# Sixteen expert groups worked in between the heads, and their routing packed into 24 heads

## The reference

```python
xn = layernorm(x)
# attention: 16 heads of 128, causal
q, k, v = xn @ Wq + bq, xn @ Wk + bk, xn @ Wv + bv
att = softmax(q k^T / sqrt(128) + causal) v      ;  att @ Wo + bo
# mixture of experts: 64 experts, the best 6 per token, at most 128 tokens per expert
scores = sigmoid(xn @ w_gate); idx = top_k(scores, 6); w = scores[idx] / sum
pos = running count of the token in its expert, over all tokens in order
x_disp[e, pos] = xn            # dropped from position 128 on
out_r = (silu(x_disp @ w_up_g) * (x_disp @ w_up_v)) @ w_down
shared = (silu(g_s) * y_s) @ w_shared_down
out = x + att + shared + sum_k w[k] * out_r[idx[k], pos[k]]
```

## Time and profile before

| | |
|---|---|
| median of three runs | 1820.65 us (1816.66 to 1821.87) |
| the profiled execution | 1822.72 us |
| its span in the trace | 1821.0 us |
| PE busy | 1690.2 us, 93% |
| DVE busy | 1368.7 us, 75% |
| ACT busy | 1085.7 us, 60% |
| POOL busy | 1122.1 us, 62% |
| mean granted PE clock | 0.956 |

### The profile page before, as it was taken

How to read it: one execution, slowest core, us unless ns; L and a number is a source line. 1 busy time by engine, 2 the same in 40 slices (tenths; PEclk the granted TensorE clock), 3 DMA queues, 4 the chain that set the end, 5 groups by cost and what they waited for, 6 DMA issues and landing times. The chain is left out here.

```text
span 1821.0 us, 49686 instructions
## 1 busy us (share of the span) xinstructions
PE 1690.2 (93%) x19217; PEld 1315.9 (72%) x19217; DVE 1368.7 (75%) x3128; ACT 1085.7 (60%) x2347; POOL 1122.1 (62%) x1006
## 2 busy tenths in 40 slices
PE   4699999999999999999986779999998999999997
PEld 3477767777777777777665667777776777777775
DVE  8677777777677777777663446888888888888885
ACT  2566666665566666666661227666666666666664
POOL 0257757776676777776660006777777677777763
PEclk7799999999999999999997669999999999999998
DMA  9377667765656665656656656778988789898976
GB/s 372 112 152 131 121 120 128 135 112 101 120 94 101 96 106 95 96 95 101 115 99 160 206 160 119 138 142 141 164 140 159 122 141 165 139 143 136 163 129 113
DMA packets 686658, 245.04 MB, mean 135 GB/s; under 512 B 637456, under 2 KB 674721, under 8 KB 685536
## 3 DMA queue, kind: packets, MB, share of 16 engines
q1 hardware_dynamic: 657472, 197.83, 61.6%
q0 software_dynamic: 18432, 33.64, 7.7%
q10 hardware_dynamic: 10528, 10.49, 1.8%
HBM read 57.11 MB, written 50.46 MB: 59 GB/s over the span
## 5 line engine op out<-in xcount | busy, mean ns | idle before, releaser
L485 POOL TENSOR_TENSOR prob<-prob 128x128 f16<-128x128 f32 (+7 forms) x512 | 653.0, 1280 | 576.1 <-ACT prob L874 569.2
L867 ACT ACTIVATE prob<-prob,nmax 128x128 f32<-128x128 f32 (+7 forms) x512 | 396.8, 775 | 530.4 <-DVE prob L1312 514.3
L708 PE MATMUL ps_s<-kT,qT 128*128 128x512 f16 (+3 forms) x2304 | 459.7, 327 | 4.3 <-DVE prob L1312 4.3
L723 PE MATMUL ps_o<-probT,vh 128*128 128x256 f16 (+1 forms) x3840 | 428.3, 265 | 7.2 <-DMA probT<-prob 7.2
L1312 DVE TENSOR_SCALAR_CACHE_REDUCE prob<-ps_s,neg_scale 128x128 f32<-128x128 f32 (+7 forms) x512 | 412.2, 809 | 14.3 <-PE ps_s L710 10.6
L723 PEld LDWEIGHTS ps_o<-probT,vh 128*128 128x128 f16 x3840 | 368.7, 99 | 53.5 <-issue 9.1
L874 ACT CAST prob<-prob 128x128 f16<-128x128 f32 (+7 forms) x512 | 341.5, 667 | 2.3
L708 PEld LDWEIGHTS ps_s<-kT,qT 128*128 128x128 f16 x2304 | 201.9, 98 | 144.7 <-issue 4.3
L1341 DVE SCALAR_TENSOR_TENSOR resid<-ps_y,yscale,resid 128x256 f32<-128x256 f32 x512 | 223.0, 477 | 11.6 <-PE ps_y L737 5.8
L737 PE MATMUL ps_y<-wo,oT 128*128 128x256 f16 x1536 | 210.6, 273 | 22.2 <-DVE oT L1327 20.4
L599 PEld LDWEIGHTS ps_t<-xT,wq 128*128 128x128 f16 x6144 | 205.1, 100 | 24.6 <-issue 9.8
(11 more groups left out here) (182 smaller groups left out, 1651.6 us busy)
## 6 DMA issues: line engine op xcount, KB each, us to landing
dispatched<-zeros SPq DMA_DIRECT2D x16, 512.0 KB, 14.1
probT<-prob SPq DMA_TRANSPOSE x512
ex<-dispatched SPq DMA_DIRECT2D x16, 512.0 KB, 4.3
expert_out<-eo ACTq DMA_DIRECT2D x16, 512.0 KB, 3.7
eup<-in_L_ffn_w_up_dram SPq DMA_DIRECT2D x64, 64.0 KB, 2.1
dispatched<-xn,slot_idx POOLq DMA_INDIRECT x192
xn_columns<-xnth SPq DMA_DIRECT2D x24, 128.0 KB
got<-expert_out,slot_idx POOLq DMA_INDIRECT x192
```

The costliest lines, as they stand in the source:

```text
L485: pool.tensor_tensor(low_cols(j), prob_cols(j).rearrange("p (r k) -> p r k", k=P), high_cols(j), ALU.subtract).then_inc(p_low, 1)
L708: pe.matmul(s_cols(j, lo, hi), qT[:, u, a, j * P:(j + 1) * P], kT[:, u, c, lo:hi], start=(n == 0), stop=(n == 2 and hi < w))
L723: mm = pe.matmul(ps_o[:, lo:2 * P], vh[:, u, a, r * D:(r + 1) * D], probT[:, PT_AT[c] + 2 * r + s, lo:], start=(r + n == 0), stop=(r == 2 ...
L867: nc.scalar.activation(prob_cols(j), prob_cols(j), ACT.Exp, bias=nmax[:, j:j + 1], scale=-1.0, accum_out=rsum[:, i % 2, j:j + 1]).then_inc ...
```

## The change

The loop of its own for the experts goes away, on all engines; every engine calls `attention(0, B * H)` once. `early(i)` and `later(i)` place the work: group pair e = i - 27 starts in head i, and ends in head i + 1.

```diff
-        ROWS = 2 * NP
-        SPLIT = ROWS + 2
+        ROWS = 3 * NP // 2
+        NGR = E // EG
+        EX0 = ROWS + 3
+        GA0 = EX0 + NGR // 2 + 1
         def even_part(i):
-            return i // 2 if i % 2 == 0 and i < ROWS else -1
+            return 2 * (i // 3) + i % 3 if 0 <= i < ROWS and i % 3 < 2 else -1
         def odd_part(i):
-            return i // 2 if i % 2 == 1 and i < ROWS else -1
+            return 2 * (i // 3) + i % 3 - 1 if 0 <= i < ROWS and i % 3 > 0 else -1
...
+        def early(i):
+            return i - EX0 if EX0 <= i < EX0 + NGR // 2 else -1
+        def later(i):
+            return i - EX0 if EX0 < i <= EX0 + NGR // 2 else -1
```

PE's order in the expert heads (lines without a + stood there before):

```diff
                     scores(i, 1)
+                    if later(i) >= 0:
+                        hidden_columns(i, 2 * later(i) - 2)
+                        up_project(i, 2 * later(i) - 1)
...
                         project_y(i - 1, 1)
+                    if early(i) >= 0:
+                        rows_to_columns(i, 2 * early(i), 0)
+                    if old:
                         values(i - 1, 2)
                     scores(i, 3)
+                    if early(i) >= 0:
+                        rows_to_columns(i, 2 * early(i), 1)
...
                         project_y(i - 1, 2)
+                    if even_part(i) >= 0 and even_part(i) % 2:
+                        transpose_rows(i, even_part(i))
+                    if mid_part(i) >= 0:
+                        shared_down(i, mid_part(i))
+                    if later(i) >= 0:
+                        down_project(i, 2 * later(i) - 2, 0)
+                        down_project(i, 2 * later(i) - 2, 1)
...
                     scores(i, 5)
+                    if later(i) >= 0:
+                        hidden_columns(i, 2 * later(i) - 1)
+                    if early(i) >= 0:
+                        up_project(i, 2 * early(i))
+                        rows_to_columns(i, 2 * early(i) + 1, 0)
...
                     scores(i, 6)
+                    if later(i) >= 0:
+                        down_project(i, 2 * later(i) - 1, 0)
...
                     scores(i, 7)
+                    if early(i) >= 0:
+                        rows_to_columns(i, 2 * early(i) + 1, 1)
+                    if later(i) >= 0:
+                        down_project(i, 2 * later(i) - 1, 1)
```

The new PE functions borrow PSUM from the attention, and wait for it. Three of the four `rows_to_columns` halves write ps_y, which `project_y` uses:

```diff
+            def rows_to_columns(i, n, h):
+                dst = ps_t[:, 0, :] if n % 2 + h == 0 else ps_y[:]
+                if n % 2 + h:
+                    pe.wait_ge(y_added, NC * (i - 1) + 2 * (n % 2) + h + 1)
...
+            def hidden_columns(i, n):
+                pe.wait_ge(eh_ready, n + 1)
+                if n % 2:
+                    pe.wait_ge(eo_d, n)
+                else:
+                    pe.wait_ge(y_added, NC * (i - 1) + 1)
...
+            def down_project(i, n, h):
+                bank = (n + h) % 2
+                if n % 2 == 0:
+                    free_bank(i, bank)
...
+                pe.matmul(ps_t[:, bank, :], ehT[two, n % 2, :], edn[two, :], start=True, stop=True).then_inc(ed_done, 1)
```

More of the change, by code:

```diff
@@ L257, in causal_attention_with_moe @@
         eo_d = sem("eo_d")
-        eo_stored = sem("eo_stored")
+        eo_out = [sem(f"eo_out{h}") for h in range(2)]
         gathered = [sem(f"gathered{u}") for u in range(2)]
@@ L627, in project_v @@
                 h = i % H
+                if half == 0 and early(i) >= 0 and not turn(i, more):
+                    pe.wait_ge(eta_ready, 2 * early(i) + 1)
                 if i == 0 and half == 0:
@@ new lines, in up_project @@
+            def up_project(i, n):
+                if n % 2:
+                    pe.wait_ge(y_added, NC * (i - 1) + 1)
+                elif n:
+                    pe.wait_ge(eo_d, n - 1)
+                else:
+                    free_bank(i, 1)
+                pe.wait_ge(eup_in, 16 * EG * (n + 1))
+                pe.wait_ge(eta_ready, n + 1)
+                pe.wait_ge(etd_ready, n + 1)
+                dst = ps_y[:, 2 * P:] if n % 2 else ps_t[:, 1, 2 * P:]
+                for e in range(EG):
+                    for k in range(KC):
+                        mm = pe.matmul(dst[:, e * 2 * HE:(e + 1) * 2 * HE], exT[:, e, k, :], eup[:, e, k, :],
+                                       start=(k == 0), stop=(k == KC - 1))
+                mm.then_inc(eu_done, 1)
@@ L729, in project_y @@
                 pe.wait_ge(o_low, m + 1)
+                if c == 0 and early(i) >= 0:
+                    pe.wait_ge(etd_ready, 2 * early(i) + 2)
+                if c == 1 and later(i + 1) >= 0:
+                    pe.wait_ge(eht_ready, 2 * later(i + 1) - 1)
+                    pe.wait_ge(eu_taken, 2 * later(i + 1))
+                if c == 2 and early(i + 1) >= 0:
+                    pe.wait_ge(etd_ready, 2 * early(i + 1) + 1)
+                if c == 3 and early(i + 1) >= 0:
+                    pe.wait_ge(eta_ready, 2 * early(i + 1) + 2)
                 if m:
@@ L972, in attention @@
                         high_q(i + 1, 1)
+                    if later(i) >= 0:
+                        gate_of_hidden(2 * later(i) - 1)
+                    if early(i) >= 0 and i > EX0:
+                        load_expert_rows(2 * early(i) + 1)
                     softmax_exp(i, 2)
@@ L975, in attention @@
                         high_weights(3)
+                    if early(i) >= 0:
+                        first_columns(2 * early(i))
                     if old:
@@ L1401, in attention @@
                         low_q(i + 1, 1)
-                    if late >= 0:
-                        slot_indices(late)
+                    if later(i) >= 0:
+                        hidden(2 * later(i) - 1)
+                    if i == EX0 - 1:
+                        gate_weights()
+                    if slot_part(i) >= 0:
+                        slot_indices(slot_part(i))
                     if odd >= 0:
@@ L1432, in attention @@
                         add_y(i - 1, 2, mixed(4))
+                    if even >= NC and even % 2:
+                        low_columns(even)
+                    if mid_part(i) >= 0:
+                        add_shared(mid_part(i), NC * (i - 1) + 3)
+                    if later(i) >= 0:
+                        second_outputs(2 * later(i) - 2)
+                    if old:
                         low_o(i - 1, 3)
@@ L1438, in attention @@
                         low_k(i + 1, 0)
-                    if even >= NC:
+                    if early(i) >= 0:
+                        hidden(2 * early(i))
+                    if even >= NC and even % 2 == 0:
                         low_columns(even)
@@ L1449, in attention @@
                     block_max(i, 7)
+                    if early(i) >= 0:
+                        second_columns(2 * early(i) + 1)
+                    if later(i) >= 0:
+                        second_outputs(2 * later(i) - 1)
                     mix_at(7)
```

490 lines of the change are left out of this document (266 added, 224 removed).

## The result

The changed kernel takes 1873.41 us (median of 4 runs, 1871.78 to 1876.38), the kernel before 1819.89 beside it: a ratio of 1.030, 95% interval 1.028 to 1.032. It is slower, as forecast, but 42 us over the forecast of 1831 and 17 beyond the range's end. The profiled execution took 1872.88 us with a span of 1871.1; 1872.88 - 1822.72 = 50.2 us have to be explained.

A forecast was written before the change was run, and what follows sets the result against it. PE was taken to be full wherever there are heads, leaving room only in the expert phase, drain and refill. Terms -135.9 + 73 + 33 - 4 + 24 + 18 + 2 = +10.1 gave 1831 us median, range 1796 to 1856.

The forecast's parts named there:

- Term 1: Heads 33 and 34 with the expert phase between: drain, expert work and refill go, -135.9 us.
- Terms 2 and 3: Expert heads: the experts' own PE time returns, +73 us; new in-order PE waits, mostly for DVE, +33 us.
- Point (2): Heads 28 to 34 take 36.6 us plus a clock drop each, some 38; under 34 refutes the added waits.
- Point (3): PE idles ahead of a transposing matmul reading ex, released by DVE, 2 to 3 us, seven or eight times.
- The turn at head 31: Head 31 already waits for columns; the 2.5 us wait and added transposes lie under that transfer, -4 us.
- Terms 4 and 5: Routing in 24 heads: new PE waits, +24 us (-8 to +45); some 12 clock drops, +18 us (0 to 30).
- term 6: Additions, gathers and statistics: a ninth addition per head hidden by slack, statistics squeezed into six heads; +2 us.
- Point (5): Clock entries of 0.5 in the expert heads and triples of routing heads, 10 to 16 of them.
- Rival 1: The clock holds: same waits, but no drop follows; -18, 1813 us; chance 0.17.
- The lock on DVE: `hidden`, with both operands in SBUF, may be slowed while POOL works; 0.3 us taken, 0 to 1.5 per head.
- Rival 2: Waits for add_y and low_v are hidden: 1756 us with none, 1781 with a third; chance 0.15.
- Rival 3: Longer chains: two more us in each of 9 expert and 16 routing heads, less catch-up, +25, 1856 us; chance 0.18.

The follow-up runs named there:

- experiment 3: Changed kernel, but PE issues 32 unused products ahead of the wait for POOL's normalised rows in six routing heads; 1850.79 us, ratio 1.0198.
- experiment 1: Changed kernel, but POOL normalises an odd pair's two tiles behind low_probs 1 and 2 instead of 2 and 3; 1846.75 us, ratio 1.0143.
- the fastest variant: Three-edit kernel of experiment 6, plus ACT copying v and odd pairs' columns earlier and DVE taking low_v earlier; 1776.31 us, ratio 0.9792.
- Experiment 5: Changed kernel, but routing as in the kernel before, experts behind heads 35 to 43, twelve additions per late head; 1829.23 us, ratio 1.0061.
- experiment 6: Changed kernel with POOL's normalise earlier, shared down product behind values, odd group's hidden rows later, and add_shared ahead of add_y(i-1, 2); 1806.76 us, ratio 0.9932.

## Why the prediction was wrong, point by point

**Term 1, the phase (-135.9): right.** No long stretch at low clock is left.

**Terms 2 and 3, the expert heads (+73 and +33): right.** The nine heads cost 115.3 more than plain ones; four drops at 1.6 are 6.5 of it, which leaves 35.8 for the waits beside the 73 of work. Point (2) said 36.6 us for a full head and 38 with a drop: 36.66 and 38.2 to 38.9. Point (3): 2.3 us seven times where I had 2.5. Behind scores 1 it is 0.6 as worked out, behind scores 7 0.7 for 1.1; heads 27 and 35 wait for more than the 4 together. That the total of a full head came out to 0.1 is in part luck: PE waits for 3.6 where I had 4.2, and its own time is larger by about as much (33.05 us busy, against 23.50 + 9.1). All waits of the nine heads in the trace add up to 31.6, so some 4 us of the 35.8 are not waits.

**The turn at head 31 (-4): right.** A turn cost 4.2 above its neighbours (30.03 against 25.86); it now takes 38.55 against 38.25.

**Terms 4 and 5, routing (+24) and the clock (+18): here the forecast broke.** The sum was +10, measured are +50. Routing cost 70.4 + 4.2 (the turn's saving is in the 70.4) = 74.6 us, of which I split off the clock as follows. Between heads 1 and 35 the trace has 105.8 us at half clock, as much as 31 stretches of 3.41; 27 of them lie in routing heads. The price of one is 1.6 (38.25 - 36.66), of two running together 2.4 to 2.85 (experiment 3): by this estimate some 38 us (36 to 40) in routing heads, less 3 for the two that the kernel before had there, and 6.5 in expert heads. So term 4 proper is 74.6 - 35 = 40 in place of 26 (with the 2 of term 6 for statistics), and term 5 is some 41 in place of 18. The miss of 40 is thus about 14 of idle in routing, 23 of clock, and 3 more in the expert heads.

*The idle* is one sentence of term 4: "Now transposes (head 3m+1) and shared_down (3m+2) stand right there and need that bank". The transposes need the bank *and* the normalised rows. I followed who frees the destination and not who makes the source. The triples of 25.3, 28.3 and 29.3 are right without that and without the clock: 25.5; 28.6 in experiment 1; 31.17 less 1.7 is 29.5. PE idles for 3.8 in place of 1.8 in six heads, but the 1.3 that I had for k vanished beneath it. Without the clock such a head takes 28.64 + 3.80 - 2.86 = 29.6 (experiment 1) in place of 28.3, so this makes 8 of the 14 us. The other 6 lie in the other routing heads and were not taken apart. The bound of +45 held.

*The clock* is the larger part. Its form was right, idles of PE bring stretches at half clock, but I counted one stretch for each of some 12 idles, and there were 31: heads 3m+1 and 3m+2 together brought 10.2 us per triple, three stretches' worth, where I had one or two. POOL's wait caused a good part of that: the six heads had ten of the stretches and without it have none (experiment 1), and putting it back into the fastest variant brought about 12 us of clock. The bound of 30 for this term allowed no more than some twenty stretches at 1.6, and that is why the range ended too low. The expert heads had four drops and not some seven. Point (5) said 10 to 16 entries; heads 1 to 35 have 21, twelve of 3.41 us and nine longer ones. Rival 1 asked whether the wait behind scores 3 brings a drop, which was the smaller question.

**Term 6 (+2): right.** Late heads take 23.6 us with nine additions, and the statistics cost about as much as before, packed into six heads or not (some 5 us above the neighbours now, some 4 before).

**The lock on DVE: small.** One of the four operations of `hidden` takes 0.65 in place of 0.29 us in eight of its sixteen cases, 0.36 more in one of the two groups of a head; I had taken 0.3.

**Rival 2, the waits are hidden (1756 to 1781): wrong for this kernel, and yet reachable.** The mended kernel's 0.979 lies at its upper end. The Trainium skill's "Perfetto Trace Analysis", section "Optimization Strategy", says that interleaving regimes with different bounds may improve performance. Experiment 5 and the booking above agree with that for the phase alone: 135.9 us became 115.3, and 1.3 to 2.9 us less per full head once `hidden` had moved. The same section says that a bubble which keeps recurring on the engine that should be full may come from too few buffers for the next tile. Here the measurement says otherwise: the bubbles of 3.8, 2.3 and 1.8 us recurred 6, 7 and 8 times, and all of them shrank or went by reordering, without another buffer; whether one more buffer would have done the same was not tried.

**Rival 3 (1856, the chains are longer)** had the right sign and named no place. 17 us more than it gave came true, through a link that it didn't name and the clock behind it.

## What to carry to other kernels

When a step moves earlier in an in-order stream, list everything that it waits for, its sources as well as its destination, and look up for each when it is done today, above all for those that nobody waits for now. Then ask what stands in front of the producer in *its* stream. Price an idle of the matrix engine with the clock that follows: here one of 3.8 us cost some 6.2 to 6.7.

## What the runs showed of the hardware

The half-clock stretches don't follow the length of an idle alone. In the changed kernel the same idle of 2.31 us came with one in heads 29 and 33 and with none in heads 28, 30, 32 and 34. The 1.80 of heads 3m+2 came with 3.41 or 6.83 us each time there, while in experiment 1 head 8 had the same 1.80 and none. With the three edits made (experiment 6) the 1.80 of heads 3m+1 brought 3.41 in two heads of six. Filling a wait with useless products kept the clock and gained 18 us, though the wait ended no sooner. Single gains overlap: 26.7 + 32.5 + 17.5 taken singly, 66.6 together. What sets off a drop stays open.

Most plain heads took 23.33 us in the three kernels that ran on one chip and 23.55 in the others, and the kernel before had a median of 1814.7 there and of 1818.0 to 1819.9 elsewhere. Differences of some 0.3% between kernels that ran on different chips thus say nothing; the ratio to the kernel before on the same chip does.
